# A tanh recurrence beside matrix products: pairs in a ring without copies, and one chain of steps per batch

## The reference, cut to what matters

```python
# x: (2, 1024, 512) f32; W_in: (1024, 512); W_out: (512, 1024); gate_w, up_w: (512, 1536); down_w: (1536, 512)
def attn(x):
    u = einsum('bsd,hd->bsh', x, W_in) + b_in
    def step(state, u_t):
        s = tanh(u_t + state * gamma + beta)
        return (s, s)
    _, states = scan(step, zeros((2, 1024)), swapaxes(u, 0, 1))
    return einsum('bsh,dh->bsd', swapaxes(states, 0, 1), W_out) + b_out

def ffn(x):   # each weight rounded to float8_e4m3fn and back
    return ((silu(x @ gate_w * gate_scale) * (x @ up_w * up_scale)) @ down_w) * down_scale

x = x + layernorm(attn(layernorm(x)))
x = x + layernorm(ffn(layernorm(x)))
```

## Time and profile before

| | |
|---|---|
| median of 3 runs | 634.06 us (633.58 to 635.42) |
| profiled execution, its own time | 634.36 us |
| its span, first to last instruction | 632.4 us |
| mean granted clock of TensorE | 0.933 |
| busy in the span | PE 527.9, DVE 489.7, POOL 306.8, ACT 293.2 us |
| 1024 scans (L634), mean | 229 ns |
| 1024 tanhs (L918), mean | 186 ns |
| GpSimd's u copies (L1006), 28 | 31.6 us |
| GpSimd's main state copies (L1016), 28 | 31.5 us |

### The profile page before, as it was taken

How to read it: one execution, slowest core, us unless ns; L and a number is a source line. 1 busy time by engine, 2 the same in 40 slices (tenths; PEclk the granted TensorE clock), 3 DMA queues, 4 the chain that set the end, 5 groups by cost and what they waited for, 6 DMA issues and landing times.

```text
span 632.4 us, 9840 instructions
## 1 busy us (share of the span) xinstructions
PE 527.9 (83%) x2880; PEld 424.5 (67%) x2880; DVE 489.7 (77%) x1832; ACT 293.2 (46%) x1354; POOL 306.8 (49%) x388
## 2 busy tenths in 40 slices
PE   4756202978999899999999999999999992999993
PEld 3744101557876897689768985898589941787992
DVE  4999997999879767876797778767886678664734
ACT  1353323345554555456545654565456544451330
POOL 2776774557544544354435443554355425243432
PEclk9957655989999999999999999999999996999997
DMA  7353341211000100010001001100001000200001
GB/s 232 127 174 109 99 163 35 83 33 51 2 1 34 68 2 0 35 67 2 2 34 67 2 2 34 47 22 1 1 29 40 1 1 2 66 2 1 2 33 34
DMA packets 16262, 27.47 MB, mean 43 GB/s; under 512 B 2000, under 2 KB 4176, under 8 KB 16208
## 3 DMA queue, kind: packets, MB, share of 16 engines
q1 hardware_dynamic: 16208, 26.83, 13.3%
HBM read 22.63 MB, written 4.19 MB: 42 GB/s over the span
## 4 chain that ended last, share of the span: by engine, by line
DVE 61%; ACT 18%; PE 11%; issue 4%; POOL 2%; DMA 1%; SPq 1%; DVEq 0%; POOLq 0%; ACTq 0%
DVE recur L634 25%; ACT pairs L918 10%; PE gate_up L529 6%; DVE fused L728 4%; ACT sigm L937 4%; DVE gated L721 3%; PE wide L554 3%; DVE peaks L780 3%; ACT fused_hi L952 3%; DVE rounder_own L776 2%; DVE z L749 2%; DVE y L675 2%; DVE rounder_own L784 2%; DVE x_norm L686 2%; DVE x_lo L698 2%
## 5 line engine op out<-in xcount | busy, mean ns | idle before, releaser
L918 ACT ACTIVATE pairs<-recur 128x16 f32<-128x16 f32 x1024 | 190.9, 186 | 273.0 <-DVE recur L634 270.0
L634 DVE TENSOR_TENSOR_SCAN recur<-recur,pairs 128x32 f32<-128x32 f32 x1024 | 234.5, 229 | 99.3 <-ACT pairs L918 97.9
L486 PE MATMUL wide<-w_out_sb,states 128*128 128x512 f32 x224 | 100.2, 601 | 39.9 <-issue 39.9
L1053 POOL TENSOR_TENSOR fused_lo<-fused,fused_hi 128x256 fp32r<-128x256 f32 x96 | 71.3, 744 | 120.1 <-ACT fused_hi L952 120.0
L472 PE MATMUL wide<-x_norm_t,w_in_sb 128*128 128x256 f32 x448 | 107.3, 397 | 13.0 <-ACT u_rows L905 6.1
L472 PEld LDWEIGHTS wide<-x_norm_t,w_in_sb 128*128 128x128 f32 x448 | 88.5, 201 | 29.8 <-ACT u_rows L905 6.9
L486 PEld LDWEIGHTS wide<-w_out_sb,states 128*128 128x128 f32 x224 | 43.0, 193 | 89.4 <-issue 88.3
L529 PE MATMUL gate_up<-x_hi,gate_q 128*128 128x256 f32 x384 | 97.1, 286 | 2.2 <-DVE fused L728 1.7
L529 PE MATMUL gate_up<-x_lo,up_q 128*128 128x256 f32 x384 | 96.1, 283 | 0.0
L529 PE MATMUL gate_up<-x_hi,up_q 128*128 128x256 f32 x384 | 95.6, 282 | 0.0
L529 PE MATMUL gate_up<-x_lo,gate_q 128*128 128x256 f32 x384 | 95.1, 281 | 0.0
(11 more groups left out here) (80 smaller groups left out, 693.5 us busy)
## 6 DMA issues: line engine op xcount, KB each, us to landing
...
raw_own<-gate_w SPq DMA_DIRECT2D x10, 256.0 KB, 2.7
raw_own<-down_w SPq DMA_DIRECT2D x9, 256.0 KB, 2.5
...
raw_own<-up_w SPq DMA_DIRECT2D x8, 256.0 KB, 2.7
w_out_sb<-w_out_t SPq DMA_DIRECT2D x8, 256.0 KB, 2.9
```

What stands on the lines that cost most here:

```text
L486: ins = eng.matmul(wide[b][:, :], states[:, j * batch + b, :], w_out_sb[:, j, :], start=(j == 0), stop=(j == KH - 1))
L634: eng.tensor_tensor_scan(preact[:, t % 2, :, :].rearrange("p c k -> p (c k)"), factors.rearrange("p c k -> p (c k)"), pairs[:, t, :, :].re ...
L918: eng.activation(pairs[:, (t + 1) % T, :, 0], preact[:, t % 2, :, 1], ACT.Tanh).then_inc(s_state, 1)
L1053: eng.tensor_tensor(fused_lo[:, f, :], fused[:, f, :], fused_hi[:, f, :].bitcast(F32), ALU.subtract).then_inc(s_fused_lo, 1)
```

## The change

Every state stays where the tanh writes it, and TensorE and ScalarE work on `pairs` directly; `states`, `u_rows`, `place_u` and `collect` go.

- `pairs` becomes a ring of 256 slots. Slot s holds the state after step s and the u of step s + 1. A block's u is written by ScalarE in strided form: `copy_u` has 16 instructions of 128 elements per block in place of 8 of 256. Where a block starts at the ring's first slot, its first u belongs to slot 255, and 8 of the 16 are split into one of 2 elements and one of 126.
- The columns are ordered by batch, and a step becomes two scans of 16 elements and two tanhs of 8: chain 0 for batch 0 at place t - 0.01, chain 1 for batch 1 at t + 0.59 (`CHAIN_BEHIND`), each with its own semaphores. Sums (`preact`) lie in SBUF, `factors` alone in PSUM.
- A y product takes 64 steps of both batches instead of 128 steps of one, its stationary operand read from `pairs` with 64 bytes between elements. Rows of x and of the output are ordered alike: row 2t + b, so each load and store of a block becomes two DMAs of every second partition.

```diff
+CHAIN_BEHIND = 0.6
...
     CH = KH * batch
+    RING = 2 * T
     TOK = batch * T
-    SLICES = 4
-    TS = T // SLICES
...
+    CHAINS = 2
+    PART = CH // CHAINS
...
-    x_blocks = x.rearrange("b (n t) d -> n t b d", t=T)
-    out_blocks = out.rearrange("b (n t) d -> n t b d", t=T)
+    x_blocks = x.rearrange("b (n g t) d -> n b t g d", g=GROUPS, t=TH)
+    out_blocks = out.rearrange("b (n g t) d -> n b t g d", g=GROUPS, t=TH)
...
-        u_rows = sb("u_rows", [P, CH, T])
-        pairs = sb("pairs", [P, T, CH, 2])
-        states = sb("states", [P, CH, T])
-        states_by_time = states[:, :, :].rearrange("p c t -> p (c t)").rearrange(
-            "p (j g b t) -> p j g b t", j=KH, g=GROUPS, b=batch)
+        pairs = sb("pairs", [P, RING, CH, 2])
+        pairs_by_batch = pairs[:, :, :, :].rearrange("p s (b j) k -> p s b j k", b=batch)
...
-        preact = recur[:, 0:2, :, :]
-        factors = recur[:, 2, :, :]
+        factors = ps("factors", [P, CH, 2])
+        preact = sb("preact", [P, CH, 2])
...
-        s_placed = sem("s_placed")
-        s_preact = sem("s_preact")
-        s_state = sem("s_state")
-        s_collected = sem("s_collected")
+        s_preact = [sem(f"s_preact{h}") for h in range(CHAINS)]
+        s_state = [sem(f"s_state{h}") for h in range(CHAINS)]
...
+        def part(h):
+            return slice(h * PART, (h + 1) * PART)
+        def state_slots(n, g):
+            first = (n * T + g * TH) % RING
+            return slice(first, first + TH)
+        def input_slots(first, last):
+            if first % RING == 0:
+                return [(0, 1, slice(RING - 1, RING)), (1, last - first - 1, slice(0, last - first - 1))]
+            at = (first - 1) % RING
+            return [(0, last - first, slice(at, at + last - first))]
...
+                    eng.dma_start(x_in[b:P:batch, :, :], x_blocks[n][b]).then_inc(s_x_in, 16)
             def load_late():
...
-                eng.dma_start(out_blocks[n], z[:, :, :]).then_inc(s_stored, 16)
+                for b in range(batch):
+                    eng.dma_start(out_blocks[n][b], z[b:P:batch, :, :]).then_inc(s_stored, 16)
...
                     eng.wait_ge(s_w_out_in, 16 * KH)
-                if b == 0:
-                    eng.wait_ge(s_collected, collected(n, SLICES - 1))
+                for h in range(CHAINS):
+                    eng.wait_ge(s_state[h], n * T + (b + 1) * TH)
                 if n < LAST:
                     eng.wait_ge(s_u_rows, KH // 2 * n + 2 + b + 1)
                 for j in range(KH):
-                    ins = eng.matmul(wide[b][:, :], states[:, j * batch + b, :], w_out_sb[:, j, :],
+                    ins = eng.matmul(wide[b][:, :],
+                                     pairs_by_batch[:, state_slots(n, b), :, j, 0].rearrange("p s b -> p (s b)"), w_out_sb[:, j, :],
                                      start=(j == 0), stop=(j == KH - 1))
                 ins.then_inc(s_y_psum, 1)
...
                 for b in range(batch):
-                    eng.tensor_copy(factors[:, b:CH:batch, 1], cols[:, 2, :]).then_inc(s_bias, 1)
-            def recurrence(n):
+                    eng.tensor_copy(factors[:, b * KH:(b + 1) * KH, 1], cols[:, 2, :]).then_inc(s_bias, 1)
+            def recurrence(n, h):
                 for t in range(T):
-                    yield t - 0.01
-                    if t % TS == 0 and n > 0:
-                        eng.wait_ge(s_placed, placed(n, t // TS))
+                    yield t - 0.01 + h * CHAIN_BEHIND
+                    if t == 0 and n > 0:
+                        eng.wait_ge(s_u_rows, KH // 2 * n)
                     elif t % TH == 0 and n == 0:
                         eng.wait_ge(s_first_u, QUADS * (t // TH + 1))
                     if t == 0 and n == 0:
                         eng.wait_ge(s_bias, 1 + batch)
                     if n + t > 0:
-                        eng.wait_ge(s_state, n * T + t)
-                    eng.tensor_tensor_scan(preact[:, t % 2, :, :].rearrange("p c k -> p (c k)"),
-                                           factors.rearrange("p c k -> p (c k)"),
-                                           pairs[:, t, :, :].rearrange("p c k -> p (c k)"), 0.0, ALU.mult,
-                                           ALU.add).then_inc(s_preact, 1)
+                        eng.wait_ge(s_state[h], n * T + t)
+                    before = (n * T + t - 1) % RING
+                    eng.tensor_tensor_scan(preact[:, part(h), :].rearrange("p c k -> p (c k)"),
+                                           factors[:, part(h), :].rearrange("p c k -> p (c k)"),
+                                           pairs[:, before, part(h), :].rearrange("p c k -> p (c k)"), 0.0,
+                                           ALU.mult, ALU.add).then_inc(s_preact[h], 1)
             def measure(w, src, n, b, halves_at, whole_at, ready):
...
-                        yield at[m] + jj
+                    for jj, g in itertools.product(range(2), range(GROUPS)):
+                        yield at[m] + GROUPS * jj + g
                         j = 2 * m + jj
-                        if jj == 0:
+                        if jj == 0 and g == 0:
                             eng.wait_ge(s_u_psum, KH // 2 * n + m + 1)
                             if m == 0 and n > 1:
-                                eng.wait_ge(s_placed, placed(n - 1, SLICES - 1))
-                        ins = eng.activation(u_rows[:, j * batch:(j + 1) * batch, :].rearrange("p b t -> p (b t)"),
-                                             wide[m % 2][:, jj * TOK:(jj + 1) * TOK], ACT.Identity,
-                                             bias=u_bias[:, j:j + 1])
+                                for h in range(CHAINS):
+                                    eng.wait_ge(s_preact[h], (n - 1) * T)
+                        for first, count, slots in input_slots(n * T + g * TH, n * T + (g + 1) * TH):
+                            at_bank = jj * TOK + g * P + first * batch
+                            ins = eng.activation(
+                                pairs_by_batch[:, slots, :, j, 1].rearrange("p s b -> p (s b)"),
+                                wide[m % 2][:, at_bank:at_bank + count * batch], ACT.Identity,
+                                bias=u_bias[:, j:j + 1])
                     ins.then_inc(s_u_rows, 1)
...
-                    yield t - 0.01
-                    if n > 0 and t == 0:
-                        eng.wait_ge(s_collected, collected(n - 1, 0))
-                    elif n > 0 and t % TS == 0:
-                        eng.wait_ge(s_collected, collected(n - 1, t // TS))
-                    eng.wait_ge(s_preact, n * T + t + 1)
-                    eng.activation(pairs[:, (t + 1) % T, :, 0], preact[:, t % 2, :, 1], ACT.Tanh).then_inc(s_state, 1)
+                    yield t - 0.01 + h * CHAIN_BEHIND
+                    if t % TH == 0 and n >= 2:
+                        eng.wait_ge(s_y_psum, batch * (n - 2) + t // TH + 1)
+                    eng.wait_ge(s_preact[h], n * T + t + 1)
+                    eng.activation(pairs[:, (n * T + t) % RING, part(h), 0], preact[:, part(h), 1],
+                                   ACT.Tanh).then_inc(s_state[h], 1)
             def split_x1(n, b, place):
...
-            def place_u(n, s, place):
-                yield place
-                ts = slice(s * TS, (s + 1) * TS)
-                if s == 0:
-                    eng.wait_ge(s_u_rows, KH // 2 * n)
-                if s == SLICES - 1:
-                    eng.wait_ge(s_state, n * T)
-                eng.tensor_scalar(pairs[:, ts, :, 1].rearrange("p t c -> p c t"), u_rows[:, :, ts], 0.0, 1.0,
-                                  ALU.add, ALU.mult).then_inc(s_placed, 1)
...
-            def collect(n, s, place):
-                yield place
-                eng.wait_ge(s_state, steps(n, s))
-                if s == 0 and n > 0:
-                    eng.wait_ge(s_y_psum, batch * n)
-                first, last = s * TS + 1, min((s + 1) * TS + 1, T)
-                if n < LAST:
-                    eng.tensor_scalar(states[:, :, first - 1:last - 1], pairs[:, first:last, :, 0].rearrange("p t c -> p c t"),
-                                      0.0, 1.0, ALU.add, ALU.mult).then_inc(s_collected, 1)
-                    if s == SLICES - 1:
-                        eng.tensor_scalar(states[:, :, T - 1:T], pairs[:, 0:1, :, 0].rearrange("p t c -> p c t"),
-                                          0.0, 1.0, ALU.add, ALU.mult).then_inc(s_collected, 1)
```

88 lines of the change are left out of this document (28 added, 60 removed).

## The result

| | before | after |
|---|---|---|
| median of 4 runs each, us | 633.82 (633.42 to 635.42) | 642.27 (642.09 to 643.19) |
| ratio of the changed kernel to the one before | | 1.013 [1.0116, 1.0145] |
| profiled execution, us | 634.4 | 642.26 |
| its span, us | 632.4 | 640.5 |

Forecast: 641, range 612 to 682, slower with a chance of 0.54. It came out slower, 1.3 us above the number.

A forecast was written before the change was run, and what follows sets the result against it. The recurrence was taken as the bound, with TensorE close behind in steady stages. 634.4 us profiled, plus 16.3 for steps, minus 9 for GpSimd copies, minus 0.8 at the end, gave 640.9, forecast as 641, range 612 to 682.

The forecast's parts named there:

- The steps: Recurrence steps: empty 0.46 us, with a 256-element filler 0.49, gate 0.54, sigmoid alone 0.57, fused_hi alone 0.50.
- The pair of scans: VectorE in a step: two 16-element scans hold it 0.10 + 0.06 = 0.16 us, bounds 0.13 and 0.26.
- The loop: One chain's scan and tanh in turn: from 0.484 us to L = 0.463, bounds 0.42 and 0.49.
- Steps with more than one ScalarE filler: Recurrence steps with two ScalarE fillers: a double copy of u takes 0.72 us, ten of them per odd steady stage.
- The copies on GpSimd: VectorE instructions stretched beside GpSimd's copies, nearly all in stages 0 and 1: about 9 us gained, bounds 6 and 11.
- The stages: Steady stages of 66 to 68 us, TensorE idle for 2 to 4; stages 0 and 1 together about 4 us shorter.
- The end: TensorE's last y product, now behind the copies, starts 0.8 us earlier.
- The sum: Whole kernel: 634.4 us profiled, plus 16.3 for steps, minus 9 for copies, minus 0.8 at the end, gives 640.9.
- Rival 1: Short recurrence instructions overlap better, filler steps at 0.46 us, and the copies decide: faster, 615.6 us; chance 0.39.
- Rival 2: Halving the recurrence's instructions saves nothing, pair 0.26 us, filler steps 0.59: much slower, 707 us; chance 0.12.
- Rival 3: TensorE's y products stall on strided weight loads at four times today's 0.19 us: about 700 us; chance 0.05.

The follow-up runs named there:

- one-chain kernel: The changed kernel with one scan of 32 and one tanh of 16 a step, sums back in PSUM: 625.06 us, ratio 0.987 to the kernel before.

## Why the prediction was right, point by point

- **The steps.** Empty 0.46 forecast, 0.467 measured; filler 0.49, 0.488 to 0.494; gate 0.54, 0.555; behind a sigmoid 0.57, 0.558; behind a fused_hi 0.50, 0.505. The form of the model held too: a step is the longest of a chain's loop, VectorE's sum and ScalarE's sum.
- **The pair of scans.** 0.16 forecast, 0.18 measured. The first term, 0.10 behind a filler, was right (0.097); the second, 0.06, was 0.08. It makes a gate step 0.555 in place of 0.54, 0.015 us on 157 gates or 2.4 us.
- **The loop.** L = 0.463, measured 0.467. Its parts: the shorter scan 30 forecast, 33 ns measured (223 to 190); SBUF write 15, measured 8 (231 to 223); SBUF read 31, measured 32 (186 to 218 for a tanh that had waited); shorter tanh 6, measured 8 (218 to 210). Errors of 7 ns one way and 3 and 2 the other mostly cancelled.
- **Steps with more than one ScalarE filler.** A double copy of u, 0.72 forecast, took 0.49 to 0.65, in the median 0.59. The forecast's ten such steps of an odd stage are seven of these and three that also hold an x_hi or a sigmoid; those took 0.79 to 1.03, and the three of an even stage 2.6 us together, not 2.3. So the two errors partly cancelled within a stage: an odd stage cost 0.7 to 0.9 us more than an even one, not 1.4.
- **The copies on GpSimd.** 9 us forecast. In stages 0, 1 and 7, VectorE's instructions other than scans have 9.0 us less above 0.5 us of duration (stage 0 15.9 to 12.1, stage 1 9.0 to 5.0, stage 7 2.1 to 0.9). The one-chain kernel's recurrence was 7.0 us shorter than before, 8.7 less in these stages and 1.7 more in the steady ones, which the sum had at nothing.
- **The stages.** Steady ones were forecast at 66 to 68 us with TensorE idle for 2 to 4 of it; they take 66.9 to 67.9 with 1.7 to 2.7. Stages 0 and 1 together were to be about 4 us shorter and are 2.5.
- **The end.** 0.8 forecast; from the last tanh's end to the end of the span 65.3 became 63.7, that is 1.6. The recurrence also began 1.1 us earlier (26.16 to 25.02), which the sum didn't have. It need not belong to the change: the kernel before with its sums in SBUF, which loads as the kernel before does, began at 24.98, and the other kernels here between 25.0 and 26.3.
- **The sum.** The recurrence grew by 10.8 us against 7.3 forecast. The one-chain kernel splits this: two chains and SBUF cost 17.9 us over it (16.3 forecast), the rest brought 7.0 (9 forecast). Start and end took 2.7 off against 0.8. So the parts were 3.5 us too low and 1.9 too high, and 641 was closer than its parts by luck, 1.1 us of it the earlier start. The costs of the common steps, which the forecast rests on, held to 0.015 us.
- **Rival 1** (the copies decide, faster). Filler steps of 0.49 against its 0.46 refute it; the pair was above 0.15. The half throughput that the Trainium skill's page "DVE: opcode table, instruction layouts, handler registers and perf-mode slots", section 6, states for this scan was good for an estimate of 33 ns for 16 elements, and the runs show 33 (scans that had waited, 223 to 190). What did not follow is the pair of 0.145: the second scan held 0.082, where a scan of 32 behind a short instruction had held 0.085, so nearly nothing was saved there.
- **Rival 2** (nothing saved by halving). Refuted for 32 to 16 elements (0.140 to 0.097 behind a filler), and for 16 to 8 as well (0.097 to 0.080), though there little is left to save.
- **Rival 3** (strided weights). The load went from 0.193 to 0.298 us, 1.5 times. The y passes are still 0.43 us apart, (4.46 - 0.59) / 9 by TensorE's timeline, so nothing waits for it:

```profile
314.45 4.46 PE L481 MATMUL wide<-w_out_sb,pairs 128*128 128x512 f32 x10
```

The Trainium skill's page "SBUF — State Buffer", section "Door 1: The DMA port swizzle", has the penalty per 16-byte line; the trace agrees and gives the size, 0.105 us a load of 128 columns at 64 bytes.

What the prediction did not say is how much of the loss a single line carries. With one chain and the sums in PSUM the same change is 8 us faster than before. The price of the read, 31 ns, stood in its working, but inside the loop of two chains; what the split costs without the move was never asked.
